# Paired narrow-tile products, earlier normalisation and a shorter VectorE list in a fused attention and expert kernel

## What is computed

```python
xn = _layernorm(x)                                  # x: 8 x 512 x 256
qkv = xn @ W_qkv.T                                  # 16 heads of 16
q_p = elu(einsum('bhnd,hdf->bhnf', q, proj)) + 1.0  # 128 features
k_p = elu(einsum('bhnd,hdf->bhnf', k, proj)) + 1.0
kv = einsum('bhnf,bhnd->bhfd', k_p, v)
attn = einsum('bhnf,bhfd->bhnd', q_p, kv)
z = 1.0 / (einsum('bhnf,bhf->bhn', q_p, k_p.sum(axis=2)) + 1e-08)
attention = (attn * z[..., None]) @ W_out.T + b_out
...
logits = xn @ Wr + br                               # 8 experts, the best 2 of a token
h = gelu(xn @ W1[e] + b1[e]); y = h @ W2[e] + b2[e] # hidden width 1024
out = x + attention + sum of y * softmax weight over the chosen experts
```

## Time and profile before

| | us |
|---|---|
| median of 3 runs | 704.22 (703.76 to 704.52) |
| the profiled execution | 703.8, its span 701.5 |
| TensorE busy | 684.2 (98%) |
| VectorE busy | 511.6 (73%) |
| ScalarE busy | 476.1 (68%) |
| GpSimd busy | 227.1 (32%) |
| first stage, up to the first expert matmul | 298 |

### The profile page before, as it was taken

How to read it: one execution, slowest core, us unless ns; L and a number is a source line. 1 busy time by engine, 2 the same in 40 slices (tenths; PEclk the granted TensorE clock), 3 DMA queues, 4 the chain that set the end, 5 groups by cost and what they waited for, 6 DMA issues and landing times.

```text
span 701.5 us, 17274 instructions
## 1 busy us (share of the span) xinstructions
PE 684.2 (98%) x5482; PEld 602.3 (86%) x5483; DVE 511.6 (73%) x1308; ACT 476.1 (68%) x875; POOL 227.1 (32%) x169
## 2 busy tenths in 40 slices
PE   8899999999999998999999999999999999999996
PEld 5676777777777776589999999999999999999996
DVE  8899989898989878848567675555767554477544
ACT  5687979796979696776567774447775444577552
POOL 1323232323232324643242432225223222322422
PEclk9999999999999999999999999999999999999999
DMA  8866474747474648865455663336646333454532
GB/s 261 203 180 170 108 227 106 226 107 226 107 227 106 197 106 226 228 180 167 78 100 137 118 167 46 46 55 102 178 66 166 50 53 52 81 125 109 69 47 22
DMA packets 87204, 91.63 MB, mean 131 GB/s; under 512 B 60049, under 2 KB 73361, under 8 KB 84897
## 3 DMA queue, kind: packets, MB, share of 16 engines
q1 hardware_dynamic: 71426, 59.36, 34.2%
q0 software_dynamic: 13872, 18.75, 15.3%
q10 hardware_dynamic: 1872, 13.11, 5.1%
HBM read 39.32 MB, written 26.67 MB: 94 GB/s over the span
## 4 chain that ended last, share of the span: by engine, by line
PE 80%; DVE 6%; issue 4%; SPq 3%; DMA 3%; ACT 2%; POOL 1%; POOLq 0%; DVEq 0%
PE F L502 9%; PE F L503 9%; PE F L504 9%; PE WK L502 5%; PE WK L504 4%; PE WK L503 4%; PE NUM L502 4%; PE NUM L504 4%; PE NUM L503 4%; PE DEN L574 4%; PE DEN L503 3%; PE DEN L502 3%; PE DEN L504 3%; PE F L565 3%; PE F L559 3%
## 5 line engine op out<-in xcount | busy, mean ns | idle before, releaser
L1864 POOL DMA_INDIRECT out<-ysb,icur x75 | 119.6, 1594 | 273.9 <-DVE ysb L1695 245.7
L1161 ACT ACTIVATE h<-F,b1c 128x384 f32<-128x384 f32 x200 | 112.2, 575 | 141.4 <-PE F L504 133.1
L1672 DVE TENSOR_TENSOR hl<-h,hh 128x768 fp32r<-128x768 f32 x100 | 96.3, 964 | 113.8 <-ACT hh L1165 113.8
L1015 ACT ACTIVATE e_ring<-F 128x512 f32<-128x512 f32 x256 | 145.3, 620 | 35.6 <-PE F L559 32.7
L502 PE MATMUL F<-gxh,wh 128*128 128x384 f32 (+1 forms) x400 | 129.1, 323 | 1.5 <-issue 1.1
L504 PE MATMUL F<-gxh,wl 128*128 128x384 f32 (+1 forms) x400 | 128.0, 320 | 0.0
L503 PE MATMUL F<-gxl,wh 128*128 128x384 f32 (+1 forms) x400 | 128.0, 320 | 0.0
L1798 POOL DMA_INDIRECT xg<-rows,slots x64 | 64.0, 1000 | 174.5 <-PE F L559 142.5
L1405 DVE SCALAR_TENSOR_TENSOR kp<-F,e_ring 128x512 f32<-128x512 f32 x128 | 82.6, 681 | 12.4 <-PE DEN L574 5.9
L1405 DVE SCALAR_TENSOR_TENSOR qp<-F,e_ring 128x512 f32<-128x512 f32 x128 | 84.9, 684 | 5.7 <-ACT e_ring L1015 4.6
L1165 ACT ACTIVATE hh<-h 128x768 fp32r<-128x768 f32 x100 | 84.7, 847 | 3.3
(11 more groups left out here) (252 smaller groups left out, 1558.3 us busy)
## 6 DMA issues: line engine op xcount, KB each, us to landing
wraw<-experts ACTq DMA_DIRECT2D x12, 1024.0 KB, 6.4
gblk<-xg SPq DMA_DIRECT2D x100, 96.0 KB
Sk<-kdh SPq DMA_DIRECT2D x64, 128.0 KB, 2.4
Sq<-qdh SPq DMA_DIRECT2D x64, 128.0 KB
xin<-x SPq DMA_DIRECT2D x8, 512.0 KB, 6.6
Sk<-kdl SPq DMA_DIRECT2D x32, 128.0 KB, 2.4
Sq<-qdl SPq DMA_DIRECT2D x32, 128.0 KB
xres<-x SPq DMA_DIRECT2D x8, 512.0 KB
```

Of the source, the lines that this page charges most:

```text
L1015: A(e_ring[:, u % 4, :], F[u % 4][:, :], ACT.Exp, bias=EXP_BIAS, scale=1.0 / DOWN).then_inc(exp_done, 1)
L1161: A(h32[:, m, :], F[m % 4][:, 0:T], ACT.Gelu, bias=b1c[:, w, m:m + 1]).then_inc(gelu, 1)
L1672: V.tensor_tensor(hl[:, 2 * q:2 * q + 2, :], h32[:, 2 * q:2 * q + 2, :], f32(hh[:, 2 * q:2 * q + 2, :]), ALU.subtract).then_inc(hl_rdy, 1)
L1864: pool.indirect_dma_start(out, bass.IndirectOffsetOnAxis(icur[:, s, :], 0), ysb[:, s, :], None, bounds_check=last_token, compute_op=ALU.ad ...
```

## The change

1. Pairs: `attend(b-1, 2)` and `attend(b-1, 3)` both follow unit 1, `attend(b, 0)` and `attend(b, 1)` unit 29, `kv(b, 0)` and `kv(b, 1)` unit 10, `kv(b, 2)` and `kv(b, 3)` unit 19. `prefix` moves from unit 30 to the end of unit 31. Some PSUM banks change.
2. Normalisation: `norm_stats` at units 12 and 13, `norm_var` at 14, nine steps (a cubic and a Newton step) in place of twelve at units 15 to 22, one block of `norm_rows` at each of units 23 to 26, all a batch earlier than the transposes need them.
3. Routing: the mask is written once, as bf16; the running sums over the token blocks are gone from VectorE (one reduction stays) and are made by three more small matmuls in `prefix`. `slots_of` moves from unit 31 to unit 2 of the next iteration, the scatters start two units later, and GpSimd's `copy_rows` goes ahead of `add_bias`. VectorE's residual 1 at unit 31 now stands ahead of `numbers_of`.
4. Start: 25 warm-up matmuls in place of 28; the first batch is transposed block by block behind its normalised rows; the rows of batch 1 are normalised before the first iteration.
5. Experts: TensorE reads the numbers of the next expert at chunk 3 of `ffn1` in every tile, into registers that two experts share in turn; the last four chunks of `ffn2` are one group in full tiles, not two.

The final iteration gets the same pair at unit 1. The diff, cut:

```diff
-WARM = 28
+WARM = 25
...
-    T_BANK = [WK[0], NUM]
+    T_BANK = [DEN, NUM]
     QK_BANK = [NUM, WK[0], WK[1], WK[0]]
     V_BANK = [WK[1], NUM, DEN, NUM]
     KV, STATE, POS = DEN, WK[0], DEN
-    ATT_BANK = [NUM, WK[0], WK[1], DEN]
+    ATT_BANK = [NUM, DEN, WK[1], WK[0]]
...
-    NORM_STEPS = 12
-    STEPS_AT = {19: (0, 1, 2), 21: (3,), 23: (4, 5, 6), 24: (7,), 25: (8,), 26: (9, 10), 29: (11,)}
+    NORM_STEPS, CUBE = 9, 0.375
+    STEPS_AT = {15: (0, 1), 16: (2,), 17: (3,), 18: (4,), 19: (5,), 20: (6,), 21: (7,), 22: (8,)}
     PIECES, PIECE = 4, 1024
-    TURN = 2
+    TURN, LATER = 2, 2
...
             nc.tensor.matmul(POS[:, 0:NT * E], tri[:, :], mskb[:, :, :], start=True, stop=False)
-            nc.tensor.matmul(POS[:, 0:NT * E], ones[:, :], cumb[:, :, :], start=False, stop=True)
+            for d in range(1, NT):
+                nc.tensor.matmul(POS[:, d * E:NT * E], ones[:, :], mskb[:, 0:NT - d, :], start=False, stop=False,
+                                 skip_group_check=True)
+            nc.tensor.matmul(POS[:, 0:NT * E], ones[:, :], cumb[:, :].unsqueeze(1).to_broadcast([P, NT, E]),
+                             start=False, stop=True)
...
+                if u == 1 and not first:
+                    pe.wait_ge(o_rdy, 2 * b - 1)
                     attend(b - 1, 2)
-                if u == 1 and not first:
-                    pe.wait_ge(pos_read, b + 1)
+                    pe.wait_ge(qkl_rdy, 4 * b + 4)
                     attend(b - 1, 3)
                 if u == 2:
-                    if not first:
-                        pe.wait_ge(att_rdy, 4 * b - 2)
+                    pe.wait_ge(pos_read, b + 1)
...
                 if u == 10:
-                    if first:
-                        pe.wait_ge(pos_read, 1)
-                    else:
+                    if not first:
                         pe.wait_ge(at_rdy, 4 * b - 2)
                     kv(b, 0)
+                    pe.wait_ge(feat, 32 * b + 8)
+                    kv(b, 1)
                 if u == 11:
-                    kv(b, 1)
                     qk_rest(b + 1, 0)
...
-                if u == 17:
-                    kv(b, 2)
                 if u == 18:
                     qk_rest(b + 1, 1)
                 if u == 19:
+                    kv(b, 2)
                     kv(b, 3)
...
                     attend(b, 0)
+                    attend(b, 1)
                 if u == 30:
                     qk_rest(b + 1, 3)
                     if not first:
                         project(b - 1, 0)
-                    prefix(b + 1)
                 if u == 31:
                     if not first:
                         pe.wait_ge(att_rdy, 4 * b + 1)
                         project(b - 1, 1)
-                    pe.wait_ge(qkl_rdy, 4 * b + 8)
-                    attend(b, 1)
+                    pe.wait_ge(att_rdy, 4 * b + 2)
+                    prefix(b + 1)
...
+        def load_numbers(e, w):
+
+            _, (first, full, end) = nc.values_load_multi_w_load_instructions(
+                tile_nums[0:1, bass.ds(e, 1), :], engines=(pe.engine,))
+            for r, v in zip(NUMS[w], (first & 127, full & 127, end & 127)):
+                pe.reg_mov(r, v)
...
+                if m == 3:
+                    load_numbers(e + 1, 1 - w)
+            late = (range(MT - 4, MT),) if n == SUB else (range(MT - 4, MT - 2), range(MT - 2, MT))
+            for chunks in (range(MT - 4), *late):
...
                 if u == 29:
+                    copy_att(b, 0)
+                    copy_att(b, 1)
+                if u == 30:
                     qk_lo(b + 1, 3)
...
         def norm_step(b, i):
 
-            y, z = rs[:, (i // 3 - 1) % 2, :], rs[:, i // 3 % 2, :]
+            seed, cubic, root = rs[:, 1, :], rs[:, 0, :], rs[:, 1, :]
             join()
             if i == 0:
                 link(V.tensor_scalar(var[:, :], mv[:, :, 1], EPS, None, ALU.add))
             elif i == 1:
-                link(V.tensor_scalar(rbits[:, :], var[:, :].bitcast(I32), 1, None, ALU.logical_shift_right))
+                link(V.tensor_scalar(seed.bitcast(I32), var[:, :].bitcast(I32), -0.5, float(0x5F3759DF), ALU.mult, ALU.add))
             elif i == 2:
-                link(V.tensor_scalar(rs[:, 0, :].bitcast(I32), rbits[:, :], -1.0, float(0x5F3759DF), ALU.mult, ALU.add))
-            elif i % 3 == 0:
-                link(V.tensor_tensor(rtmp[:, 0, :], y, y, ALU.mult))
-            elif i % 3 == 1:
-                link(V.scalar_tensor_tensor(rtmp[:, 1, :], rtmp[:, 0, :], -0.5, var[:, :], ALU.mult, ALU.mult))
+                link(V.tensor_tensor(rtmp[:, 0, :], seed, seed, ALU.mult))
+            elif i == 3:
+                link(V.tensor_tensor(rtmp[:, 1, :], rtmp[:, 0, :], var[:, :], ALU.mult))
+            elif i == 4:
+                link(V.scalar_tensor_tensor(rtmp[:, 0, :], rtmp[:, 1, :], -10.0 / 3.0, rtmp[:, 1, :], ALU.add, ALU.mult))
+            elif i == 5:
+                link(V.scalar_tensor_tensor(cubic, rtmp[:, 0, :], 5.0, seed, ALU.add, ALU.mult))
+            elif i == 6:
+                link(V.tensor_tensor(rtmp[:, 0, :], cubic, cubic, ALU.mult))
+            elif i == 7:
+                link(V.scalar_tensor_tensor(rtmp[:, 1, :], rtmp[:, 0, :], -0.5 * CUBE ** 3, var[:, :], ALU.mult, ALU.mult))
             else:
-                link(V.scalar_tensor_tensor(z, rtmp[:, 1, :], 1.5, y, ALU.add, ALU.mult))
-
-        def norm_rows(b, lo, hi):
+                link(V.scalar_tensor_tensor(root, rtmp[:, 1, :], 1.5 * CUBE, cubic, ALU.add, ALU.mult))
...
-            V.tensor_copy(cum[:, 0, :], cum[:, NT, :])
+            V.tensor_tensor(cumb[:, :], cumb[:, :], msum[:, :], ALU.add)
...
-            link(V.tensor_tensor(msk[:, :, :], lg[:, :, :], top8[:, :, 1:2].to_broadcast([P, NT, E]), ALU.is_ge))
-            join()
-            V.tensor_copy(mskb[:, :, :], msk[:, :, :])
             V.tensor_tensor(tie[:, :], top8[:, :, 2], top8[:, :, 1], ALU.is_ge)
+            V.tensor_tensor(mskb[:, :, :], lg[:, :, :], top8[:, :, 1:2].to_broadcast([P, NT, E]), ALU.is_ge).then_inc(mask_rdy, 1)
 
         def route_count(b):
 
-            for n in range(NT):
-                link(V.tensor_tensor(cum[:, n + 1, :], cum[:, n, :], msk[:, n, :], ALU.add))
-                join()
-            V.tensor_copy(cumb[:, :, :], cum[:, 0:NT, :]).then_inc(mask_rdy, 1)
+            dve.wait_ge(mask_rdy, b + 1)
+            link(V.tensor_reduce(msum[:, :], mskb[:, :, :].rearrange("p n e -> p e n"), AX_X, ALU.add))
...
-                if u == 0:
-                    norm_rows(b + 1, 0, 4)
+                if u == 2:
+                    slots_of(b)
...
                 if ahead:
-                    if u == 16:
+                    if u == 12:
                         norm_stats(b + 2, 0, 2)
-                    if u == 17:
+                    if u == 13:
                         norm_stats(b + 2, 2, 4)
                         join()
-                    if u == 18:
+                    if u == 14:
                         norm_var(b + 2)
+                    if 23 <= u < 23 + NT:
+                        norm_rows(b + 2, u - 23, u - 22)
                     for i in STEPS_AT.get(u, ()):
...
                 if u == 31:
-                    slots_of(b + 1)
+                    numbers_of(b + 1)
+                    if not ahead:
+                        slots_of(b + 1)
                 features(b, u)
...
+        norm_rows(1, 0, NT)
...
-                        pool.wait_ge(f_full, 32 * b + 1 + TURN * (2 * n + r))
+                        pool.wait_ge(f_full, 32 * b + 1 + LATER * (b < NB - 1) + TURN * (2 * n + r))
...
             send(b)
+            copy_rows(b + 1)
             add_bias(b - 1)
-            copy_rows(b + 1)
```

More of the change, by code:

```diff
@@ L132, in build @@
     top8 = sb("top8", [P, NT, 8], F32)
-    msk = sb("msk", [P, NT, E], F32)
     mskb = sb("mskb", [P, NT, E], BF16)
@@ L139, in build @@
     erec = sb("erec", [P, NT], F32)
-    cum = sb("cum", [P, NT + 1, E], F32)
-    cumb = sb("cumb", [P, NT, E], BF16)
+    msum = sb("msum", [P, E], F32)
+    cumb = sb("cumb", [P, E], BF16)
     totb = sb("totb", [P, E], BF16)
@@ L246, in build @@
     xn_rdy = sem("xn_rdy")
+    xn_first = sem("xn_first")
     xT_full = sem("xT_full")
@@ L805, in final_iteration, with first_tokens_T @@
                     attend(b, 2, ATT_LAST)
+        def first_tokens_T():
+            for n in range(NT):
+                if n < NT - 1:
+                    pe.wait_ge(xn_first, n + 1)
+                else:
+                    pe.wait_ge(xn_rdy, 1)
+                for k in range(KT):
+                    last = nc.tensor.transpose(F[k][:, n * P:(n + 1) * P], xn[:, n, k * P:(k + 1) * P], ident)
+                    if n == NT - 1:
+                        last.then_inc(xT_full, 1)
         def first_k_groups():
@@ L835, in _ @@
         pe.wait_ge(s_cst, 16)
-        for k in range(KT):
-            tokens_T(0, k, F[k])
+        first_tokens_T()
         first_k_groups()
```

(53 more changed lines are left out.)

36 lines of the change are left out of this document (15 added, 21 removed).

## The result

The changed kernel takes 723.57 us (median of 4 runs, 721.68 to 725.53) beside 703.99 us (703.08 to 704.52) of the kernel before: ratio 1.0281, 95% interval 1.0254 to 1.0307. It is slower, 2.6 us above the predicted 721.0 and inside the range. The profiled execution took 725.2 us, its span is 723.1, 21.6 more than before; the mean granted clock is 0.982, before 0.996.

What follows compares the result with a forecast made beforehand. TensorE and VectorE pull each other, with VectorE setting the pace from features 8 to unit 27. Batches 0 to 5 add 18.2 us and experts -1.0: 17.2 on 703.8 gives 721.0 us, range 709 to 733.

Steps and rivals of the forecast that it cites:

- b=0, with the start: First batch: late x landing and the statistics' earlier place cost +5.1 us, with -0.3 from the start already inside.
- b=1 to 5: Steady batches: +1.7 us each from the statistics' place, plus x waits of 0, 0.1, 1.8, 1.6, 1.1.
- b=6, 7: Last batches: pairs save 0.5 us, attend 3 waits 0.4 for features 31 behind slots_of(7); taken as 0.
- experts: Expert tiles: loading numbers at each switch's tile saves 2.0 us, loads in all tiles cost 1.0; net -1.0.
- chain from bn_stats to unit 20: VectorE's statistics ahead of features 15 delay units 16 to 19; unit 20 comes 1.85 us later, +1.7 per batch.
- Rival A: TensorE alone is the bound and VectorE's delay is absorbed: 10 us less, 694 us; chance 0.13.
- End and head of the batch: Last project matmul to unit 2: 3.25 us, attend 3 waiting 0.5 for features 31; net 0 per batch.
- x load: Load of batch b+2 lands after VectorE asks at unit 12: waits up to 1.8 us (b=3), 4 in batch 0.
- scatters two units later: GpSimd's later scatters beside the x load: no change taken, bounds -0.5 to +0.6 us each.
- rival C: As forecast, plus TensorE's clock falling in waits at units 16 to 19, 1.5 us in six batches: 730; chance 0.15.
- B: Rival: the x load doesn't bind, the statistics' place does: 713 us; chance 0.22.
- two steps 0.3 to unit 15: VectorE's first two norm steps, moved to unit 15 ahead of features 15, take 0.3 us.

Runs made afterwards that it cites:

- e10_early_x_filler: Changed kernel with x loaded half an iteration earlier and extra unused matmuls ahead of units 16 to 19: 717.30 us, ratio 1.0188.
- e3_early_x: Changed kernel with SyncE issuing the x load half an iteration earlier, ahead of the q stack DMAs: 721.54 us, ratio 1.0244.
- e2_stats_alone: Kernel before with only bn_stats moved to units 12 and 13 and bn_aggr to 14: 721.99 us, ratio 1.0255.
- e5_kv_pairs: Kernel before with only the state products paired, behind units 10 and 19: 704.89 us, ratio 1.0019.
- e11_pool_alone: Changed kernel with GpSimd's old list (scatters from unit 1, bias ahead of the copy), statistics still at unit 12: 737.62 us, ratio 1.0466.
- e7_late_and_pool: Changed kernel with statistics, norm steps and rows four units later and GpSimd's old list put back: 702.98 us, ratio 0.9993.
- e4_filler: Changed kernel with 24 extra unused matmuls per batch, after units 15 to 18: 718.65 us, ratio 1.0231.
- e8_short_bias: Changed kernel with GpSimd adding the output bias to only 8 of 256 columns: 722.02 us, ratio 1.0265.

## Why the prediction was right, and where it was wrong

The sum was 17.2 us; measured were 19.6 between the medians and 21.6 between the profiled spans, which are the ones that can be divided by its steps:

| step | forecast | span |
|---|---|---|
| b=0, with the start | 5.1 | 5.75 |
| b=1 to 5 | 1.7, 1.8, 3.5, 3.3, 2.8 | 2.3, 1.8, 4.9, 3.4, 3.3 |
| b=6, 7 | 0 | +0.9 |
| experts | -1.0 | -0.8 |

**The chain from bn_stats to unit 20 held.** Without x and clock a batch is 1.85 us longer (b=2 to 5 of e10_early_x_filler) for 1.7; in b=3 of e3_early_x unit 20 came 2.06 later (21.08 for 19.02 from unit 0) where 1.85 was worked out. e2_stats_alone shows that moving the statistics is enough to set it off. Rival A falls with it, since units 16 to 19 wait for features, and with e5_kv_pairs, where the pairs gave nothing.

**End and head of the batch held.** From the last project matmul to unit 2 it is 3.14 us (135.31 to 138.45) for 3.25, and attend 3 waits, by 0.3 us where 0.5 was said.

**The x load was mis-sized.** Issue and request fell where the sum had them: issued 9.9 us after unit 31 (10.0), asked for 15.9 after it (15.95). But the landing was taken from the earlier trace rows unchanged, 7.1 to 7.8 us, and became 5.7 to 6.6. b=3 waited 0.65 us for 1.8, all of b=1 to 5 1.2 for 4.6. The prediction named the scatters two units later as a possible cause and set it to zero. That delay is not it: in e11_pool_alone the scatters may start at unit 1 as before, and x lands as soon in b=3 to 5:

```profile
DMA to landing us min/median/max: 6.0/6.3/6.3
```

What e11_pool_alone and e7_late_and_pool (6.2 to 6.4) share with the changed kernel is `slots_of` at unit 2, by which the first scatter starts 5.4 us after unit 0 instead of 2.2. In e2_stats_alone it starts at 2.2, and x lands after 7.6 to 7.9 us in b=2 to 4, 6.5 in b=5. So the moved slots, or another part that e2_stats_alone lacks, bring x sooner; which, no run isolates.

**b=0 came out near the forecast, with a shorter wait.** The landing set the pace as the sum had it, 40.3 us for 40.6, but VectorE waited 2.15 us for the 4 foreseen, since it only got to the statistics at 38.2 instead of 36.4. Of the 5.75 us about 1.3 are a stretch at half the clock at 44.4, which was not in the 5.1.

**The clock was left out of the forecast and priced as rival C.** It happened, and about at C's price: beyond the one stretch near 30 us that both kernels have, the granted clock is 0.5 for 3.4 us in b=0, 1, 4 and 5, and for 6.8 in b=3. At the 1.3 us that one costs in e3_early_x, that makes some 7.8 us, an estimate; C had 9. That the waits of units 16 to 19 cause it is shown by e4_filler. By the Trainium skill (TensorE: Matmul & The Clock Gate, What's actually happening) activity is what lifts the throttle; the runs agree, since matmuls without use kept it lifted. So B's smaller x and C's clock held together. In the profiled execution the x waits of b=1 to 5 were 3.4 us too large in the sum, and the clock's 7.8 us were missing from it; with the smaller errors, the span came out 4.4 us above the sum. The total came that near by two errors of opposite sign, which is luck, while the chain itself was sized rightly.

**b=7 was set to zero and lost 0.8.** slots_of(7) stands ahead of features 31 as forecast, but attend 3 waits for it longer than the 0.4 that was set against the pairs:

```profile
287.87 1.07 PE L595 MATMUL WK<-qp,st_w 128*32 128x512 f32 x8
289.72 1.06 PE L595 MATMUL WK<-qp,st_w 128*32 128x512 f32 x8 [0.79 <-DVE qp L1421]
```

**Experts: the right total from two wrong halves.** The loads in the tiles cost nothing (1.0 was taken), and tiles 2 to 25 are 2.5 us shorter (2.0). The first tile is 1.7 longer, with two waits that the forecast had at 0. One is for hl, which VectorE makes behind its work on the gathered rows of the next tile; the other is at the first load of numbers, where six matmuls stand ahead of it:

```profile
340.15 0.36 PE L501 MATMUL NUM<-wh,hh 128*128 128x256 f32 x1 [1.30 <-DVE hl L1690]
341.74 0.36 PE L501 MATMUL DEN<-wh,hh 128*128 128x256 f32 x1 [0.65 <-issue]
```

**Not in the prediction at all** is GpSimd beside the norm steps. The bias beside them cost nothing as the change stands (e8_short_bias). But the term "two steps 0.3 to unit 15" rested on GpSimd being elsewhere, and the earlier trace rows alone priced it. With GpSimd's list left as it was, the same sum would have been 16.6 us too low (737.6 in e11_pool_alone for 721.0). That it wasn't is luck too.

## What to carry to other kernels

When operations of an engine are moved, look which features, units or buffers stand directly behind the new place, and what the other engines run there at that time: the same statistics are free at units 16 to 18, with GpSimd's list as it was, and cost 1.85 us a batch at 12 to 14. Leave TensorE's groups spread where it waits for VectorE, since a spread group fills its idle time: one group moved back gave 0.33 us a batch. Idle TensorE time can cost a second time through its clock; 24 useless matmuls in the gap gave about 5 us back.
